# Recommendation tower: gathers held behind the dots of a tile, and the order of batches and late halves changed

## What is computed

```python
e = stack([tbl_f[ids[:, f]] for f in range(26)])          # (512, 26, 128)
sd = einsum('bfd,bd->bf', e, dense)                        # 26 dot products per sample
ss = einsum('bfd,bgd->bfg', e, e); pairs = ss[:, iu, ju]   # 325 pairs, upper triangle
h = concatenate([dense, sd, pairs, dense], axis=1)         # (512, 607)
h = maximum(h @ W_top1 + b_top1, 0)                        # 607 -> 512
h = maximum(h @ W_top2 + b_top2, 0)                        # 512 -> 256
y = h @ W_top3                                             # 256 -> 1
```

## Time and profile before

| | us |
|---|---|
| median of 3 runs | 122.44 |
| lowest and highest of them | 114.56, 128.39 |
| the profiled execution | 114.91 |
| its span, first to last instruction | 112.6 |
| PE busy | 101.9 (90%) |
| VectorE busy | 79.4 (70%) |
| ScalarE busy | 65.9 (58%) |
| GpSimd busy | 64.2 (57%) |

### The profile page before, as it was taken

The page is one execution under the profiler, slowest core; times in us unless marked ns, Lnnn a source line. Parts: engine busy times, 40 slices in busy tenths (PEclk is TensorE's granted clock), DMA queues, the critical chain, the costliest instruction groups (busy, mean ns, idle before and its releaser), DMA issues.

```text
span 112.6 us, 2801 instructions
## 1 busy us (share of the span) xinstructions
PE 101.9 (90%) x1092; PEld 89.6 (80%) x1092; DVE 79.4 (70%) x218; ACT 65.9 (58%) x150; POOL 64.2 (57%) x66
## 2 busy tenths in 40 slices
PE   6969999979996999998899979995999969996993
PEld 6758888858775888898799868984999949996890
DVE  4699999999999999992307880888049960786002
ACT  4657489599569385692307970888049930768120
POOL 7477777777777777777777777777771000000000
DMA  3997797658999992111111221221221000000000
GB/s 91 258 256 162 202 303 217 151 151 226 288 306 292 322 313 54 41 54 52 47 52 52 67 52 47 63 63 47 52 55 38 6 0 0 6 0 0 0 0 1
DMA packets 5030, 12.35 MB, mean 110 GB/s; under 512 B 1725, under 2 KB 1853, under 8 KB 5018
## 3 DMA queue, kind: packets, MB, share of 16 engines
q1 hardware_dynamic: 2906, 8.15, 25.4%
q0 software_dynamic: 1920, 3.94, 12.9%
q10 hardware_dynamic: 192, 0.10, 0.3%
HBM read 12.18 MB, written 0.00 MB: 108 GB/s over the span
## 4 chain that ended last, share of the span: by engine, by line
PE 58%; DVE 12%; DMA 10%; ACT 7%; POOL 5%; issue 4%; SPq 1%
PE dots L470 18%; PE dots L519 14%; DVE pairs L366 11%; PE hidden L544 8%; DMA rows<-tbl,gather_idx 7%; PE hidden L470 7%; POOL rows L264 5%; ACT pairs L303 5%; DMA table<-tbl 4%; PE turned L499 3%; PE last_layers L568 2%; PE turned L544 2%; PE dots L440 1%; ACT h L344 1%; SPq L214 1%
## 5 line engine op out<-in xcount | busy, mean ns | idle before, releaser
L264 POOL DMA_INDIRECT rows<-tbl,gather_idx x60 | 61.6, 1026 | 20.1 <-issue 16.5
L366 DVE COPY pairs<-dots 27x128 f32<-27x128 f32 (+8 forms) x88 | 23.7, 269 | 17.4 <-PE dots L519 14.8
L373 DVE TENSOR_SCALAR onehot<-ids_h 125x512 fp32r<-125x512 f16 x88 | 32.4, 426 | 1.0 <-ACT ids_h L309 1.0
L303 ACT COPY pairs<-dots 27x128 f32<-27x128 f32 (+8 forms) x88 | 21.0, 238 | 18.8 <-PE dots L519 16.8
L470 PE MATMUL dots<-onehot,high 125*128 125x512 f32 (+1 forms) x64 | 22.9, 382 | 0.0
L470 PE MATMUL dots<-onehot,low 125*128 125x512 f32 (+1 forms) x64 | 21.6, 363 | 0.0
L319 ACT CAST high<-table 125x1024 fp32r<-125x1024 f32 (+1 forms) x12 | 11.8, 982 | 11.3 <-DMA table<-tbl 5.4
L519 PEld LDWEIGHTS dots<-embT 128*64 128x64 f32 x512 | 15.5, 138 | 2.2 <-issue 2.1
L519 PE MATMUL dots<-embT 128*64 128x54 f32 x512 | 16.0, 223 | 1.3 <-DVE pairs L366 0.7
L381 DVE TENSOR_TENSOR low<-table,high 125x512 fp32r<-125x512 f32 x22 | 14.9, 678 | 0.0
L544 PE MATMUL hidden<-pairs,wp 128*128 128x128 f32 x112 | 13.4, 277 | 0.8 <-ACT pairs L303 0.8
(11 more groups left out here) (52 smaller groups left out, 101.8 us busy)
## 6 DMA issues: line engine op xcount, KB each, us to landing
table<-tbl SPq DMA_DIRECT2D x10, 448.0 KB
wp<-w_pairs SPq DMA_DIRECT2D x2, 512.0 KB
rows<-tbl,gather_idx POOLq DMA_INDIRECT x60, 2.6
table<-tbl SPq DMA_DIRECT2D x10, 52.0 KB
wd<-w_dense SPq DMA_DIRECT2D x1, 512.0 KB
w2s<-w SPq DMA_DIRECT2D x1, 512.0 KB
table<-tbl SPq DMA_DIRECT2D x2, 224.0 KB
denseT<-dense_t SPq DMA_DIRECT2D x1, 256.0 KB, 4.1
```

What stands on the lines that cost most here:

```text
L264: pool.indirect_dma_start(out=rows[:, t % 2, n, :], out_offset=None, in_=tables[GATHERED_TABLES[n]][:, :], in_offset=bass.IndirectOffsetOn ...
L303: return nc.scalar.copy(dst, src)
L366: return nc.vector.tensor_copy(dst, src)
L373: nc.vector.tensor_scalar(onehot[:, i % STAGES, c, :], ids_h[:, i % ID_BUFFERS, :], float(c), None, ALU.is_equal).then_inc(onehot_ready, 1)
```

## The change

The gathers wait otherwise: 32 for the dots of tile 0, 41 for those of tile 1, 51 for those of tile 2; the two other dictionaries go. In the list, the first halves `T9.0` and `T10.0` come together, ahead of the last two batches of tile 1, and `D0` follows; both late halves come behind `D0`, their copies are steps of their own (`A9`, `A10`). Several early batches come one table later. `B2.0` and `B2.1` stand ahead of `D1`, `B2.2` and `B2.3` ahead of layer 1 of tile 0. `W14` is gone. `Y` and the relu of layer 2 are split into a step of TensorE and a step of the copying engines (`H`, `V`), and `Y0` and `Y1` come behind `D2` and `D3` instead of ahead of them. Batches take banks by a string, `BATCH_BANKS`, in turns; the last batch of tile 3 goes to the first bank of the dots. `spread_ids(3)` comes behind table 0 instead of ahead of it.

```diff
@@ -59,7 +59,7 @@
-    HELD_BY_DOTS, HELD_BY_BATCH, HELD_BY_LAYER1 = {40: 1, 51: 2}, {46: 10, 48: 11, 53: 12}, {55: 1, 57: 2}
+    HELD_BY_DOTS = {32: 1, 41: 2, 51: 3}
@@ -177,19 +177,21 @@
-                 "M": "layer2", "Y": "layer3", "W": "warming"}
+                 "M": "layer2", "H": "relu2", "Y": "layer3", "V": "result", "A": "late half"}
         STEPS = [(NAMES[w[0]], *map(int, w[1:].split("."))) for w in """
-            T0 T1 B0.0 T2 B0.1 T3 B0.2 T4 B0.3 T5 B1.0 T6 T7 B1.1 T8 B1.2 T9.0 B1.3 T9.1 T9.2
-            T10.0 B2.0 T9.3 T9.4 D0 C0.0 T10.1 T10.2 T10.3 T10.4 C0.1 P0 B2.1 P1 W14 B2.2
-            D1 C1.0 B2.3 L0.0 L0.1 R0 C1.1 B3.0 M0 Y0
-            D2 C2.0 B3.1 L1.0 L1.1 R1 C2.1 P2 B3.2 M1 B3.3 Y1
-            D3 C3.0 L2.0 L2.1 R2 C3.1 P3 M2
-            L3.0 Y2 L3.1 R3 M3 Y3""".split()]
-
-        PLACERS = [0, 0, 0, 0, 0, 0, 0, 0, 1, 0, 1, 0, 1, 0, 1, 1]
-
-        APART = 2 * BATCHES + 2
-        BESIDE = (1, 3, 5)
+            T0 T1 B0.0 T2 B0.1 T3 T4 B0.2 T5 B0.3 T6 B1.0 T7 T8 B1.1 T9.0 T10.0 B1.2 B1.3
+            D0 C0.0 T9.1 T9.2 T9.3 T9.4 A9 T10.1 T10.2 T10.3 T10.4 C0.1 P0 B2.0 B2.1 A10
+            D1 C1.0 B2.2 B2.3 L0.0 L0.1 R0 C1.1 P1 M0 H0 B3.0
+            D2 Y0 C2.0 V0 B3.1 L1.0 L1.1 R1 C2.1 P2 B3.2 M1 H1 B3.3
+            D3 Y1 C3.0 V1 L2.0 L2.1 R2 C3.1 P3 M2 H2
+            L3.0 Y2 V2 L3.1 R3 M3 H3 Y3 V3""".split()]
+
+        PLACERS = [0, 0, 0, 0, 0, 0, 0, 1, 0, 1, 0, 1, 1, 1, 0, 1]
+
+
+        BATCH_BANKS = "TLTLTLTLTLTLTTTD"
+        BEFORE_LATE = BATCH_BANKS.rindex("L", 0, 2 * BATCHES)
+        LAST_IN_L = BATCH_BANKS.rindex("L")
@@ -255,10 +257,6 @@
                     if k in HELD_BY_DOTS:
                         pool.wait_ge(dots_done, HELD_BY_DOTS[k])
-                    if k in HELD_BY_BATCH:
-                        pool.wait_ge(transposed, HELD_BY_BATCH[k])
-                    if k in HELD_BY_LAYER1:
-                        pool.wait_ge(layer1_done, HELD_BY_LAYER1[k])
@@ -267,7 +265,8 @@
         def transposes_of(n):
-            return last_layers[:, :].rearrange("p (a b) -> p a b", a=BATCH_T) if n == APART or n in BESIDE else turned
+            bank = {"L": last_layers[:, :], "D": banks[0]}.get(BATCH_BANKS[n])
+            return turned if bank is None else bank.rearrange("p (a b) -> p a b", a=BATCH_T)
@@ -446,11 +445,8 @@
             def step(kind, t, i=0):
-                if kind == "warming":
-                    pe.wait_ge(table_placed, N_ONEHOT + 1)
-                    warm(t)
-                elif kind == "table" and i == 0:
-                    if t + IDS_AHEAD < N_ONEHOT:
+                if kind == "table" and i == 0:
+                    if 0 < t < N_ONEHOT - IDS_AHEAD:
                         spread_ids(t + IDS_AHEAD)
@@ -472,10 +468,12 @@
                     last.then_inc(table_selected, 1)
+                    if t == 0:
+                        spread_ids(IDS_AHEAD)
                 elif kind == "table":
                     if t == N_ONEHOT - 2 and i == 1:
-                        placer = batch_placer(max(BESIDE))
-                        pe.wait_ge(batch_placed[placer], placed_by(placer, max(BESIDE) + 1))
+                        placer = batch_placer(BEFORE_LATE)
+                        pe.wait_ge(batch_placed[placer], placed_by(placer, BEFORE_LATE + 1))
@@ -489,12 +487,16 @@
                     pe.wait_ge(gathered[t % 2][i], 16 * BATCH_SIZE[i] * (t // 2 + 1))
-                    if n == APART:
-                        pe.wait_ge(table_placed, N_ONEHOT + 1)
-                    elif n >= 2:
-                        previous = n - 2 if n == APART + 1 or n <= max(BESIDE) + 1 else n - 1
+                    bank = BATCH_BANKS[n]
+                    if bank == "D":
+                        for engine in range(2):
+                            pe.wait_ge(pairs_copied[engine], ALL * t)
+                    elif bank in BATCH_BANKS[0:n]:
+                        previous = BATCH_BANKS.rindex(bank, 0, n)
                         placer = batch_placer(previous)
                         pe.wait_ge(batch_placed[placer], placed_by(placer, previous + 1))
+                    if bank == "L" and n > BEFORE_LATE:
+                        pe.wait_ge(table_placed, N_ONEHOT + 1)
...
```

More of the change, by code:

```diff
@@ L330, in step @@
                     nc.scalar.copy(embT[:, samples, t], selected[t % STAGES][:, samples]).then_inc(table_placed, 1)
-                elif kind == "table" and i == 4:
+                elif kind == "late half":
                     act.wait_ge(table_selected, t + 1 + len(late))
@@ L345, in step @@
                                              ).then_inc(h1_ready, 1)
-                elif kind == "layer2":
+                elif kind == "relu2":
                     act.wait_ge(layer2_done, CHUNKS2 * t + 1)
@@ L410, in step @@
                                             ALU.add, ALU.max).then_inc(h2_ready[1], 1)
-                elif kind == "layer3":
+                elif kind == "result":
                     dve.wait_ge(layer3_done, t + 1)
@@ L548, in step @@
                     if t == 0:
-                        placer = batch_placer(APART)
-                        pe.wait_ge(batch_placed[placer], placed_by(placer, APART + 1))
+                        placer = batch_placer(LAST_IN_L)
+                        pe.wait_ge(batch_placed[placer], placed_by(placer, LAST_IN_L + 1))
                     else:
```

## The result

The changed kernel takes 130.49 us (median of four executions). The ratio to the kernel before is 1.132, 95% interval 1.113 to 1.151: 13% slower. The profiled execution took 130.39 us with a span of 128.6.

The account below looks back on a forecast made before the run. VectorE's one-hot tiles were taken to bound the tables, then a per-tile cycle of dots and copies. Span 112.6 - 4.6 + 2.7 - 0.4 + 5.4 + 4.7 + 0.5 = 120.9; plus 2.31 and clock 4.7: 127.9 us, range 120 to 134.

Parts of the forecast that it names:

- (a): Rival: the same waits between dots, but TensorE's clock stays up; 123.2 us, chance 0.20.
- (b): Rival: D0 doesn't start early but at 55.6; 132.5 us, chance 0.12 shared with slower executions over 130.
- (c): Rival: held gathers issue quicker; at 0.6 us each with the clock kept, 112.8 us; chance 0.05.
- (d): Rival: holds don't bind, as gathers 32, 41, 51 reach GpSimd's front late anyway; some 110.8 us, chance 0.04.
- How this stands to the runs: Sum is for an execution like the profiled one, 7.5 us under the 122.44 median; the range's high end covers others.
- Tables, -4.6: Before the first dots: TensorE's waits go, VectorE's one-hot tiles set the floor; D0 starts at 50.95 instead of 55.60.
- D0 to D1, 9.5 us: Tile 0's dots to tile 1's: gather 32 waits for D0, B2.1 needs gather 37; 9.5 instead of 6.8, +2.7.
- D1 to D2, 14.0: Gather 41 waits for D1, B2.3 needs gather 44, then layer 1, relu, copies; 14.0 instead of 8.5, +5.4.
- D2 to D3, 14.0: Tile 2's dots to tile 3's: gather 51 waits for D2, B3.3 needs gather 59; 14.0 instead of 9.3, +4.7.
- Tail, +0.5: After D3: Y1 stands ahead of layer 1 of tile 2, and relu and second copies wait behind it; +0.5 us.
- Clock, +4.7, two pieces of work at half rate: Behind TensorE's holes the clock falls; two pieces of work lose 2.35 us each, bounds nothing and 7 us.
- The prediction's 130.2: Time if each hole counts by the Trainium skill's clock rule: 123.2 plus 7 us.

Follow-up runs that it names:

- experiment 3: Changed kernel, holds kept, with empty matmuls filling TensorE's holes ahead of B2.1, B2.2, B2.3 and behind tile 2's dots: 126.65, 126.82 and 125.69 us.
- experiment 7: Kernel before without any of its six holds: one execution of 113.47 us at full clock, three others of 122.46, 122.60 and 129.68 us.
- 6: Changed kernel with only its third hold (gather 51 behind the dots of tile 2): 117.02 us.
- 2: Kernel before, order unchanged, with gathers 34, 42 and 51 held behind the dots of tiles 0, 1 and 2, other holds gone: ratio 1.183.
- experiment 9: Kernel before with VectorE's lead over TensorE cut by one table: ratio 1.000, longest executions 119.4, 123.4 and 124.4 us.
- 1: Changed kernel with no gather held behind dots, all else as changed: 110.67 us, ratio to the kernel before 0.977.
- 8: Changed kernel with gather 41 held by tile 0's dots and 51 by tile 1's, 32 not held: 110.77 us, ratio to the kernel before 0.979.
- 10: Changed kernel without holds and with VectorE's lead cut by one table: 110.74 us, ratio to the kernel before 0.980.

## Why the forecast was right and wrong

**The mechanism held.** Slower, by gathers held behind dots, with a lower clock behind the holes; and the time, 130.5, lies in the range around 127.9. Rivals (a) to (d) fell: the clock did fall (experiment 3), D0 was early, the gather pace after a pause is 1.25 us as ever, the holds bind.

**The failed step** is "How this stands to the runs". It set the sum beside the median of 122.44 and left what the longer executions carry without a price ("the trace doesn't show what the others carry"). Read so, the change is forecast at +5.5 us or 4.5%, where 13% was measured. The sum was made for an execution like the profiled one, 114.91 us, and over that its +13.0 us is 11.3%. The runs showed that this was the right base: the kernel before took 114.56 and 115.09 us in the measurement of the result, and 112.2 to 115.4 in every execution of the experiments that kept a granted clock of 0.999 or more, while the long ones have a clock of 0.946 to 0.985 and, where a close relative was traced, one gather of 15 us (experiment 7).

**The mis-sized terms** of the sum made it 3.0 us of span short, some 2 in the waits and 0.9 in the clock; the largest difference is on the way from D1 to D2:
- *Tables, -4.6*: was -4.1. The floor was VectorE, as said; the last one-hot tile was finished 0.3 us later than in the trace of before. The transposes of B1.2 and B1.3 didn't hide under ScalarE's copy but ended 0.1 behind it, for 0.2 us more than forecast.
- *D0 to D1, 9.5 us*: was 10.6. Gather 32 started 0.8 us behind the dots instead of 0.3, and B2.1 took 1.04 at the lower level. The other two gathers behind a hold started 0.28 behind their dots.
- *D1 to D2, 14.0*: was 17.0. Layer 1 took 5.92 at the lower level instead of 3.6, B2.3's transposes took 0.3 more, and they began 2.68 us after the issue of gather 44 instead of 2.42.
- *D2 to D3, 14.0*: was 14.9, by another path. Gather 59 landed about 105.6, but the last batch goes to a bank of the dots, free only when all copies of tile 2 are done (106.2), and these waited for the relu behind the slow layer 1. The prediction had layer 1 "fit under it"; with the clock low it didn't.
- *Tail, +0.5*: was +0.6.
- *Clock, +4.7, two pieces of work at half rate*: the rows give 1.85 in the dots, 0.9 in transposes, 2.2 in layer 1 of tile 0 and about 0.7 by that of tile 1, 5.6 in sum; filling gave 3.8 to 4.7. The size was nearly right, the place partly: D3 ran at 3.94, and layer 1 of tile 1, not counted, was slow instead.

ScalarE's row behind "done (106.2)", the second copies of tile 2:

```profile
103.44 2.75 ACT L302 COPY pairs<-dots 23x32 f32<-23x32 f32 x11
```

GpSimd's pauses were forecast at 5, 2 and 5 us and came at 8.8, 5.0 and 8.8. That alone cost nothing, since each way between dots is counted from the end of the dots and not from when the gather reaches the front.

On the rule of the Trainium skill ("TensorE: Matmul & The Clock Gate", "Why this matters for your kernels", against idle stretches between bursts): the trace agrees for three of the four holes, by the granted clock of 0.65, 0.61 and 0.68. The fourth, ahead of D3, hardly opened (idle for 0.45 and 0.94 us), and the clock stayed; in experiment 3 it fell at the same place behind 0.95 and 0.94 us, which a rule on long idle stretches doesn't cover. The prediction's 130.2, three pieces of work at 2.35 us each, comes within 0.3 us of the measured time by luck: one of its three, D3, cost nothing, and the waits were some 2 us longer than it had them. That transposes don't keep the clock up (Part 4 of that page of the Trainium skill) fits the seven in the longest hole, but no run separates it from idling.

## What to carry to other kernels

A hold on an in-order queue delays everything behind it, by the queue's own pace: before adding one, work out when the held item reaches the front, and when the last item that the next step needs would then land. Here three such waits at 1.25 us a gather cost 15 us and the holes a further 4 to 5 by the clock, while the order that they came with is worth 2% alone. And give a forecast change against executions of the kind that the sum was made for: a median over a few that differ by 12% is no base.

## What the runs showed of the hardware

**A gather that sticks.** In the four profiled executions that came out long, a single gather occupies GpSimd for 19.17 us (experiment 3), 19.16 (6), 15.27 (7) and 9.66 us (2), where it is otherwise 0.94 to 1.36. GpSimd of experiment 7, then VectorE of the same execution:

```profile
21.70 1.34 POOL L264 DMA_INDIRECT rows<-tbl,gather_idx  x1 [0.31 <-issue]
23.35 15.27 POOL L264 DMA_INDIRECT rows<-tbl,gather_idx  x1 [0.30 <-issue]
38.93 0.94 POOL L264 DMA_INDIRECT rows<-tbl,gather_idx  x1 [0.30 <-issue]
```

```profile
36.10 0.70 DVE L381 TENSOR_TENSOR low<-table,high 125x512 fp32r<-125x512 f32 x1
36.70 1.10 DVE L373 TENSOR_SCALAR onehot<-ids_h 125x512 fp32r<-125x512 f16 x3
51.05 0.76 DVE L373 TENSOR_SCALAR onehot<-ids_h 125x512 fp32r<-125x512 f16 x2 [13.24 <-PE hidden L470]
```

The gather ends at 38.62, 0.82 us after VectorE's stream stops at 37.80 for want of TensorE, which itself waits for that gather. The same in experiments 3 and 6: VectorE stops at 41.40 and 41.29, the gather ends at 42.22 and 42.10. In experiment 2 VectorE first pauses because its one-hot tiles are all made, not for want of anything that hangs on the gather, and the gather ends 0.81 us after that pause begins:

```profile
41.41 9.66 POOL L264 DMA_INDIRECT rows<-tbl,gather_idx  x1 [2.27 <-PE dots L470]
```

```profile
49.58 0.68 DVE L400 TENSOR_TENSOR wd<-wd 128x512 f32<-128x512 f32 x1
50.41 0.91 DVE L402 MEMSET pairs<- 32x1024 f32 x1 [0.16 <-issue]
```

So in all four the gather ends 0.81 or 0.82 us after the first break in VectorE's stream, nearly the whole length of an ordinary gather, whatever caused the break. The Trainium skill ("SBUF — State Buffer", "SBUF: two separate sides") describes such a case: GpSimd writes the descriptors of its DMAs through ports that it shares with VectorE, and can't while VectorE runs an operation of a mode that takes both. The ends agree with that. No run shows that VectorE's operations here are of that mode, why the lock would outlast single ones, or why it does so in some executions and not in others, and experiment 9 didn't settle whether a shorter stream helps. It may account for the spread of the kernel before from 114.6 to 128.4 us; no long execution of that kernel itself was traced. The order without binding holds (experiments 1, 8 and 10) had no such execution in 16; as three of 21 executions of the held kernels with the same tables came out at least 14 us longer, that may be chance.

**Its follow-up cost is the clock.** In experiments 3, 6 and 7 TensorE then waits 13.10, 12.58 and 14.46 us for the gather's batch. The granted clock is 0.59 to 0.60 from 36 to 52 us and 0.922 to 0.939 over the span, where their other executions had 0.986 to 1.000, 0.970 to 0.985 and 0.972 to 1.000. In experiment 2, where the wait for the batch is 4.87 us, it is 0.903 against 0.913 to 0.948.
